# Shared expert over four PSUM banks each way, its down product three batches behind the gate

## The chip, the cores and the metric

The kernel runs on one NeuronCore of a Trainium2 chip. The core has five engines that matter here: TensorE (PE, matrix products, in the profile split into matmuls, PE, and weight loads, PEld), VectorE (DVE), ScalarE (ACT), GpSimd (POOL) and SyncE (SP, which only issues DMAs). Each engine works through its own list of instructions in order; semaphores order the engines against each other. PE writes its results to PSUM, eight banks of 512 fp32 numbers in each of 128 partitions; DVE and ACT read them from there. The metric is device microseconds from the start to the end of one execution.

## The reference

The input x has 32 batches of 128 tokens with 128 features. Four residual steps follow each other: a cross-attention with 16 heads of 8 features, a mixture of 8 experts (two per token), a cross-attention with 16 heads of 64 features, and a mixture of 16 experts (one per token) beside a shared expert that every token passes through. The change touches only the shared expert of the last step:

```python
logits = x @ w_router.T
_, top_idx = jax.lax.top_k(logits, 1)
...
expert_out = jnp.einsum('eth,ehf->etf', ...)        # the one expert that a token chose
shared = jax.nn.silu(x @ w_gate.T) * (x @ w_up.T) @ w_down.T
out = shared + expert_out.sum(axis=0)
```

Here x is the normalised input of the step, w_gate and w_up have 256 rows, and w_down turns 256 features back into 128.

## The kernel before

The program is written out by hand: every engine has one list, and the order in a list is the order of the calls in the source. P is 128, NB is 32 (the batches), LAST is 31. The stages follow each other: the first attention (to about 200 us in the trace), its experts (to 340), the second attention (to 745), the shared expert together with the routing of the second mixture (to 811), and the expert tiles (to the end).

**The shared expert, one batch b.** PE runs shared_gate(b) (line 1450): four fp32 matmuls of 128x128 into one PSUM bank, s_bank[b % 2]; the trace shows them as eight records, because an fp32 matmul is two instructions. The first two matmuls are the gate, the other two the upward product. ACT runs its own shared_gate(b) (line 1885): silu of the first half of the bank into sg[b % 2]. DVE runs product(b) (line 2443): sg times the second half of the bank into hT[b % 2]. PE runs shared_down(b) (line 1462): two matmuls (four records) from hT into the bank st_bank[1 - b % 2]. DVE runs add_shared(b) (line 2451): it adds that bank to x[:, b, :]. GpSimd then scatters the 128 rows of the batch with one indirect DMA (line 965) to buf1 in HBM, each row to the slot of its expert.

**The semaphores between them** are counters: g_full (gate done), sg_done (silu), sh_done (product), sy_full (down product), sy_done (sum). need(engine, semaphore, value) waits only for a positive value. Since there are two banks, gate b waits until the product of b-2 has read its bank, and down product b waits for the sum of b-2.

**The order of PE.** drain() (line 1485) ends the second attention and places the first gates and down products between the last transposes and logits. last_ranks() counts tokens per expert into the banks of and jf. Then a loop runs shared_gate(b) and shared_down(b - 2) for b from 4 to 33. Behind it PE runs warm(SCATTER_WARM), 20 matmuls whose result nobody reads, waits until all 32 scatters have landed (scattered), and runs warm(LOAD_WARM), eight more. Both write to the bank of.

**The order of DVE.** In drain() (line 2486) stand product(0) to product(2) among the norms and the choice of experts, then expert_slots() (line 2533) with product(3), add_shared(1), add_shared(2) and the arithmetic that gives each token its slot, then the loop product(b), add_shared(b - 1) for b from 4, and for b = 16 to 20 one step of tile_experts (line 2551) ahead of the product. expert_slots reads the banks of and jf.

**Behind the stage.** SP loads a quarter of the down weights of the experts, over the normalised rows xnFT, after each eight gates (line 729), and loads the first expert tiles from buf1 once all scatters have landed (line 731). DVE scales a tile by its score, PE transposes it, and the expert tiles begin: 47 of them, each with the same 8 and 4 matmul records as a batch here and one transpose, and one indirect DMA of GpSimd that stores it.

**Banks.** bank[0] to bank[3] are the four banks of sf, bank[4] and bank[5] the two of mf, and of and jf are a bank each. s_bank is bank 0 and 1, st_bank is bank 2 and 3, pj_bank is bank 4 and 5. The second bank of mf holds transposes and logits up to DVE's choose_last, which stands before product(2).

Of the kernel before, what the change touches and what calls it, by code (L numbers as in the profile page):

```python
# [9 lines left out]
ALU = mybir.AluOpType  # L10
ACT = mybir.ActivationFunctionType
AX = mybir.AxisListType

NB = 32
# [259 lines left out]
XRING, YRING, XSEMS = 20, 8, 6  # L274
DEEP = 4
XPARTS = 4
XB = NB // XPARTS
# [4 lines left out]
LAG0 = X0 + 4  # L282
DRAIN0 = 4


# [4 lines left out]
def build(nc, a, out):  # L290
    ctx = ExitStack()
    with ctx:
# [128 lines left out]
        xsT1 = [xsT[r // 2][:, r % 2, :] for r in range(DEEP)]  # L421
        hT1 = [hT[r // 2][:, :, (r % 2) * P:(r % 2 + 1) * P] for r in range(DEEP)]
        ysb1 = [rows[:, XRING + r, 0:DM] for r in range(YRING)]
        W0 = F0 + 2
# [28 lines left out]
        o_bank = [of[:, 0:QH * (D1 + 1)], mf[:, 0, 0:QH * (D1 + 1)]]  # L453
        g_bank, y_bank = bank[0:4], (of[:, 0:DM], jf[:, 0:DM])


# [85 lines left out]
        with nc.Block(no_gpsimd_drain=True) as block:  # L542
# [437 lines left out]
            def _(pe):  # L980
# [469 lines left out]
                def shared_gate(b):  # L1450

                    if b == 0:
                        pe.wait_ge(M1.w_in, 32)
                        pe.wait_ge(L1.exp_done, 2 * NB)
                    pe.wait_ge(L1.moved_done, MOVED1[b + 2] + 1)
                    need(pe, M1.sh_done, b - 1)
                    for c in range(4):
                        last = nc.tensor.matmul(s_bank[b % 2][:, c * P:(c + 1) * P], wgu[:, c * P:(c + 1) * P], xnFT[:, b, :],  # L1458
                                                start=True, stop=True)
                    last.then_inc(M1.g_full, 1)  # L1460

                def shared_down(b):
# [3 lines left out]
                    pe.wait_ge(M1.sh_done, b + 1)  # L1466
                    need(pe, M1.sy_done, b - 1)
                    for c in range(2):
                        last = nc.tensor.matmul(st_bank[1 - b % 2][:, 0:DM], hT[b % 2][:, c, 0:P], wdn[:, c, :], start=(c == 0),
                                                stop=(c == 1))  # L1470
# [14 lines left out]
                def drain():  # L1485
# [26 lines left out]
                    last_ranks()  # L1512
                    for b in range(4, NB + 2):
                        if inside(b):
                            shared_gate(b)
                        shared_down(b - 2)

# [86 lines left out]
                pe.wait_ge(slots_ready, NROUNDS + 3)  # L1604
                warm(SCATTER_WARM)
                pe.wait_ge(M1.scattered, 16 * NB)
                warm(LOAD_WARM)

# [36 lines left out]
            def _(act):  # L1645
# [239 lines left out]
                def shared_gate(b):  # L1885

                    act.wait_ge(M1.g_full, b + 1)
                    need(act, M1.sh_done, b - 1)
                    nc.scalar.activation(sg[b % 2][:, :, :], s_bank[b % 2][:, 0:2 * P], ACT.Silu).then_inc(M1.sg_done, 1)

# [88 lines left out]
            def _(dve):  # L1979
# [463 lines left out]
                def product(b):  # L2443

                    dve.wait_ge(M1.sg_done, b + 1)
                    need(dve, M1.sy_full, b - 1)
                    nc.vector.tensor_tensor(hT[b % 2][:, :, 0:P], sg[b % 2][:, :, :],
                                            s_bank[b % 2][:, 2 * P:4 * P].rearrange("p (c n) -> p c n", c=2),
                                            ALU.mult).then_inc(M1.sh_done, 1)

                def add_shared(b):

                    dve.wait_ge(M1.sy_full, b + 1)
                    nc.vector.tensor_tensor(x[:, b, :], x[:, b, :], st_bank[1 - b % 2][:, 0:DM], ALU.add).then_inc(M1.sy_done, 1)

# [30 lines left out]
                def drain():  # L2486
# [31 lines left out]
                    for b in range(4, NB):  # L2518
                        if NB // 2 <= b <= NB // 2 + 4:
                            tile_experts(b - NB // 2)  # L2520
                        product(b)
                        add_shared(b - 1)
                    add_shared(LAST)

# [220 lines left out]
```

## Time and profile before

| | us |
|---|---|
| median of three timed runs | 844.25 |
| lowest and highest | 844.01, 845.23 |
| span of the profiled execution | 913.6 |
| PE busy in it | 839.1 |
| DVE busy | 600.8 |
| ACT busy | 553.3 |
| POOL busy | 474.1 |

For the profiled execution only the span is known, from its first to its last instruction; it is longer than the timed runs. Each row of the trace has a start, a duration, the engine, the line of the source, the operation with output and inputs, and in brackets how long the engine had been idle before it and who released it. Starts on PE are recorded, the ends of matmuls are modelled. A row with x8 is eight instructions in a row, one overlapping the next. Indirect DMAs appear on POOL as the time that GpSimd needs to issue them; their landing is later.

### The profile page before, as it was taken

Reading aid. Unit: us, or ns where it says so; the run is one execution under the profiler, and the core shown is the slowest. Engines: PE = TensorE matmul, PEld = TensorE weight load, DVE = VectorE, ACT = ScalarE, POOL = GpSimd, SP = SyncE. Lnnn points to the kernel's source line nnn. Section 1 sums busy time; section 2 is a strip of 40 time slices with the busy share of each in tenths; the row PEclk is TensorE's granted clock in tenths of the full one; section 3 lists DMA queues with packets and bytes.
Section 4 is the critical chain, followed back from the end, with each engine's and each line's share of the span. In section 5 each row is a group of like instructions: output and inputs, shape, how many; then the busy total and the mean of one; then the engine's idle time right before and its main releaser. Section 6 shows DMA issues by size and latency. Waiting matters only on the chain.

```text
span 913.6 us, 31471 instructions
## 1 busy us (share of the span) xinstructions
PE 839.1 (92%) x11905; PEld 715.4 (78%) x11905; DVE 600.8 (66%) x1729; ACT 553.3 (61%) x1221; POOL 474.1 (52%) x575
## 2 busy tenths in 40 slices
PE   8998888878899998999999999999999998888786
PEld 3666555546589987998998998998999998867686
DVE  8886677734565647887777777677777676424343
ACT  4886676535387775776665666666666652225463
POOL 6333323463614436786656656655654444544455
PEclk9998999978799998999999999999999999999999
DMA  5455553513534432333553001001000002343330
GB/s 155 137 160 155 157 158 120 154 39 137 195 100 131 129 99 88 107 116 79 175 200 141 24 24 31 24 26 31 23 25 20 12 2 65 115 154 96 92 104 25
DMA packets 84148, 87.37 MB, mean 96 GB/s; under 512 B 15057, under 2 KB 70552, under 8 KB 83234
## 3 DMA queue, kind: packets, MB, share of 16 engines
q1 hardware_dynamic: 74946, 68.11, 24.7%
q0 software_dynamic: 8256, 17.01, 6.0%
q8 instruction: 99, 1.62, 0.7%
q14 instruction: 47, 0.39, 0.1%
q10 hardware_dynamic: 800, 0.24, 0.1%
HBM read 43.13 MB, written 40.44 MB: 91 GB/s over the span
## 4 chain that ended last, share of the span: by engine, by line
PE 81%; DVE 9%; issue 4%; ACT 2%; another core or an unknown queue 1%; DMA 1%; POOL 1%; SPq 0%; ACTq 0%; DVEq 0%; POOLq 0%
PE of L1367 8%; PE sf L1321 7%; PE jf L1242 6%; PE sf L1630 5%; PE sf L1283 4%; PE sf L1559 4%; PE mf L1269 4%; DVE cmx L2004 4%; PE jf L1251 3%; PE sf L1547 3%; PE sf L1458 3%; PE sf L1251 3%; PE of L1080 3%; PE sf L1033 2%; PE mf L1348 2%
## 5 line engine op out<-in xcount | busy, mean ns | idle before, releaser
L882 POOL TENSOR_TENSOR pl<-pT,ph 128x512 bf16<-128x512 f32 x128 | 146.1, 1165 | 105.1 <-DVE ph L2272 101.2
L806 POOL DMA_INDIRECT buf<-gu,slots x64 | 63.8, 996 | 88.9 <-PE of L1169 38.4
L2278 DVE TENSOR_REDUCE cmxb<-mf 128x8 bf16<-128x1024 f32 x64 | 78.2, 1222 | 43.6 <-PE mf L1348 39.2
L1700 ACT ACTIVATE pTf<-sf 128x1024 f32<-128x1024 f32 x64 | 62.6, 1022 | 36.6 <-PE sf L1040 18.0
L2004 DVE TENSOR_REDUCE cmx<-mf 128x8 bf16<-128x1024 f32 x64 | 78.1, 1220 | 10.0 <-PE mf L1061 6.8
L1818 ACT ACTIVATE pT<-sf 128x1024 f32<-128x1024 f32 x64 | 66.6, 1041 | 25.1 <-PE sf L1331 25.1
L1321 PE MATMUL sf<-qTs,kTs 64*128 64x128 f32 x1024 | 75.0, 286 | 1.6 <-ACT pT L1818 1.6
L871 POOL DMA_INDIRECT gb<-eo,slots x64 | 64.9, 1014 | 19.0 <-issue 18.9
L971 POOL DMA_INDIRECT out<-rows x47 | 46.3, 984 | 50.7 <-DVE rows L2677 39.7
L1321 PEld LDWEIGHTS sf<-qTs,kTs 64*128 64x128 f32 x1024 | 62.6, 188 | 7.1 <-issue 2.1
L1242 PE MATMUL jf<-wo,oT 128*128 128x128 f32 x496 | 62.9, 280 | 0.0
L1242 PEld LDWEIGHTS jf<-wo,oT 128*128 128x128 f32 x496 | 57.8, 192 | 0.0
L2263 DVE TENSOR_TENSOR o1s<-of,rden 128x256 f32<-128x256 f32 x125 | 53.1, 425 | 4.3
L1080 PE MATMUL of<-pTf,vq 128*32 128x128 f32 x1024 | 41.4, 290 | 12.6 <-issue 7.5
L1923 ACT ACTIVATE hT<-sf,qTs 128x128 f32<-128x128 f32 x142 | 44.6, 367 | 13.0 <-PE sf L1547 10.6
L2669 DVE TENSOR_TENSOR hT<-kTs,sf 128x256 f32<-128x256 f32 x47 | 19.8, 421 | 47.4 <-ACT kTs L1973 40.7
L1630 PE MATMUL sf<-xsT,qTs 128*128 128x128 f32 x376 | 49.7, 275 | 0.0
L861 POOL DMA_DIRECT2D eo<-rows x35 | 19.6, 561 | 52.2 <-DVE rows L2605 52.2
L1782 ACT CAST kTb<-mf 128x512 bf16<-128x512 f32 x24 | 14.1, 586 | 53.9 <-PE sf L1269 53.9
L1559 PE MATMUL sf<-dn,hT 128*128 x284 | 44.4, 279 | 1.9 <-DVE rows L2605 1.4
L1630 PEld LDWEIGHTS sf<-xsT,qTs 128*128 128x128 f32 x376 | 45.6, 191 | 0.0
L1547 PE MATMUL sf<-qTs 128*128 128x128 f32 x284 | 44.4, 279 | 0.1
(353 smaller groups left out, 2725.4 us busy)
## 6 DMA issues: line engine op xcount, KB each, us to landing
buf<-zero SPq DMA_DIRECT2D x12, 516.0 KB, 7.1
rows<-buf SPq DMA_DIRECT2D x47, 129.0 KB
buf<-zero SPq DMA_DIRECT2D x22, 256.0 KB, 3.8
eo<-zero SPq DMA_DIRECT2D x22, 256.0 KB
ctxT<-in_ctxP SPq DMA_DIRECT2D x24, 192.0 KB, 2.4
rows<-buf SPq DMA_DIRECT2D x71, 64.0 KB
gu<-in_gu SPq DMA_DIRECT2D x4, 1024.0 KB
kept<-kTs SPq DMA_DIRECT2D x6, 512.0 KB
```

The source lines that it names most:

```text
L871: nc.gpsimd.indirect_dma_start(out=gb[t % 4 * 2 + k][:, :], out_offset=None, in_=eo0[0:ZROW + P, :], in_offset=bass.IndirectOffsetOnAxis(a ...
L882: nc.gpsimd.tensor_tensor(pl[h][:, :, c, :], pT[h][:, :, c, :], ph[h][:, :, c, :], ALU.subtract)\
L1080: last = nc.tensor.matmul(of[32 * c:32 * c + 32, j * P:(j + 1) * P], vq[q % 2][:, u, h, :], pTf[p][:, h, :], start=True, stop=True)
L1242: last = nc.tensor.matmul(ps[:, 0:DM], oT[:, c, :], wo1[:, c, :], start=(c == 0), stop=(c == NCH - 1))
L1321: nc.tensor.matmul(S1[:, r, n * P:(n + 1) * P], kT[p][rr, 4 * h + n, :], qT[p][rr, 4 * h + n, :], start=(n == 0), stop=False)
L1367: last = nc.tensor.matmul(ps[:, j * (D1 + 1):(j + 1) * (D1 + 1)], pp[h][:, r, n, :], va1[p][part][:, QH * g + j, :], start=(m == 0), stop= ...
L1547: last = nc.tensor.matmul(s_bank[n % 2][:, f * P:(f + 1) * P], stage0[n % DEEP][:, f * P:(f + 1) * P], xsT0[n % DEEP], start=True, stop=True)
L1559: last = nc.tensor.matmul(st_bank[n % 2][:, 0:DM], hT1[n % DEEP][:, f, :], w2r[:, bass.ds(e, 1), f, :].squeeze(1), start=(f == 0), stop=(f ...
L1630: last = nc.tensor.matmul(g_bank[n % DEEP][:, c * P:(c + 1) * P], stage[n % DEEP][:, c * P:(c + 1) * P], xsT1[n % DEEP], start=True, stop= ...
L1818: nc.scalar.activation(pT[h][:, :, :, :].rearrange("p r c n -> p r (c n)"), S1, ACT.Exp, scale=D1 ** -0.5)\
L2004: nc.vector.reduce_max(to, mf[:, :, :].rearrange("p c (j k) -> p c j k", j=QH), AX.X)\
L2278: nc.vector.reduce_max(cmx1[b % 2][:, :].rearrange("p (r k) -> p r k", r=2)[:, :, 4 * h:4 * h + 4], M1p[:, :, :].rearrange("p r (c k) -> p ...
```

## The change

The gates get four PSUM banks and the down products four others, with slots that follow the batch number modulo four from batch 4 on and modulo two before. Products and silus get four buffers each: hT1, which the expert tiles use too, and sgs, the two old sg and two parts of pT[1]. The waits are counted accordingly: gate b waits for product b-4, from batch 8 on (6 and 7 wait for product 2). In PE's loop the down product stands three batches behind the gate. DVE adds batch b-3 behind product b, and the last three at the end; for b = 4 and 5 it adds nothing. The warm-up matmuls go to bank 0, since of is now a bank of the down products.

```diff
+BEHIND = 3
+def shared_slot(b):
+    return b % 4 if b >= 4 else b % 2
+def shared_before(b):
+    return b - 4 if b >= 8 else 2 if b >= 6 else b - 2
...
+        sgs = [t[:, :, :] for t in sg] + [pT[1][:, r, 0:2, :] for r in range(2)]
+        gs_bank = s_bank + pj_bank
+        sy_bank = [t[:, 0:DM] for t in (st_bank[1], st_bank[0], of, jf)]
...
-                    need(pe, M1.sh_done, b - 1)
+                    need(pe, M1.sh_done, shared_before(b) + 1)
                     for c in range(4):
-                        last = nc.tensor.matmul(s_bank[b % 2][:, c * P:(c + 1) * P], wgu[:, c * P:(c + 1) * P], xnFT[:, b, :],
+                        last = nc.tensor.matmul(gs_bank[shared_slot(b)][:, c * P:(c + 1) * P], wgu[:, c * P:(c + 1) * P], xnFT[:, b, :],
...
-                    need(pe, M1.sy_done, b - 1)
+                    need(pe, M1.sy_done, shared_before(b) + 1)
                     for c in range(2):
-                        last = nc.tensor.matmul(st_bank[1 - b % 2][:, 0:DM], hT[b % 2][:, c, 0:P], wdn[:, c, :], start=(c == 0),
+                        last = nc.tensor.matmul(sy_bank[shared_slot(b)], hT1[b % DEEP][:, c, :], wdn[:, c, :], start=(c == 0),
...
-                    for b in range(4, NB + 2):
+                    shared_gate(4)
+                    shared_down(2)
+                    shared_gate(5)
+                    for b in range(6, NB + BEHIND):
                         if inside(b):
                             shared_gate(b)
-                        shared_down(b - 2)
+                        shared_down(b - BEHIND)
...
-                warm(SCATTER_WARM)
+                warm(SCATTER_WARM, bank[0])
                 pe.wait_ge(M1.scattered, 16 * NB)
-                warm(LOAD_WARM)
+                warm(LOAD_WARM, bank[0])
...
-                    need(act, M1.sh_done, b - 1)
-                    nc.scalar.activation(sg[b % 2][:, :, :], s_bank[b % 2][:, 0:2 * P], ACT.Silu).then_inc(M1.sg_done, 1)
+                    need(act, M1.sh_done, b - DEEP + 1)
+                    nc.scalar.activation(sgs[b % DEEP], gs_bank[shared_slot(b)][:, 0:2 * P].rearrange("p (c n) -> p c n", c=2),
+                                         ACT.Silu).then_inc(M1.sg_done, 1)
...
-                    need(dve, M1.sy_full, b - 1)
-                    nc.vector.tensor_tensor(hT[b % 2][:, :, 0:P], sg[b % 2][:, :, :],
-                                            s_bank[b % 2][:, 2 * P:4 * P].rearrange("p (c n) -> p c n", c=2),
+                    need(dve, M1.sy_full, b - DEEP + 1)
+                    nc.vector.tensor_tensor(hT1[b % DEEP], sgs[b % DEEP],
+                                            gs_bank[shared_slot(b)][:, 2 * P:4 * P].rearrange("p (c n) -> p c n", c=2),
...
-                    nc.vector.tensor_tensor(x[:, b, :], x[:, b, :], st_bank[1 - b % 2][:, 0:DM], ALU.add).then_inc(M1.sy_done, 1)
+                    nc.vector.tensor_tensor(x[:, b, :], x[:, b, :], sy_bank[shared_slot(b)], ALU.add).then_inc(M1.sy_done, 1)
...
                         product(b)
-                        add_shared(b - 1)
-                    add_shared(LAST)
+                        if b >= 2 * BEHIND:
+                            add_shared(b - BEHIND)
+                    for b in range(NB - BEHIND, NB):
+                        add_shared(b)
```

## Rows read from the trace of the kernel before

**Rows 1.** The first line of the page: the span of the profiled execution.

```profile
span 913.6 us, 31471 instructions
```

**Rows 2.** Busy us by stretch: PE, PEld, DVE, ACT, POOL (instructions), PE clock, DMA share, GB/s.

```profile
400.00:744.00 344.00, 342.85 (x6154) 313.08 (x6147) 253.05 (x674) 222.24 (x458) 202.31 (x223) 1.00 0.20 60
763.00:811.00 48.00, 41.34 (x353) 39.53 (x351) 23.14 (x78) 10.94 (x29) 28.90 (x30) 1.00 0.34 113
820.00:911.00 91.00, 71.99 (x610) 68.48 (x608) 38.71 (x138) 48.06 (x137) 45.47 (x47) 1.00 0.31 86
```

**Rows 3.** In order of time, 773 to 780: PE, then ACT, DVE and POOL.

```profile
773.47 1.13 PE L1458 MATMUL sf<-dn,wgu 128*128 128x128 f32 x8 [1.01 <-DVE hT L2447]
774.43 0.61 PE L1469 MATMUL sf<-wdn,hT 128*128 128x128 f32 x4
...
776.22 1.06 PE L1458 MATMUL sf<-dn,wgu 128*128 128x128 f32 x8
777.11 0.61 PE L1469 MATMUL sf<-wdn,hT 128*128 128x128 f32 x4
...
774.63 0.38 ACT L1889 ACTIVATE sg<-sf 128x256 f32<-128x256 f32 x1 [1.46 <-PE sf L1458]
...
778.33 0.38 ACT L1889 ACTIVATE sg<-sf 128x256 f32<-128x256 f32 x1 [1.87 <-issue]
...
775.08 0.29 DVE L2454 TENSOR_TENSOR rows<-rows,sf 128x128 f32<-128x128 f32 x1 [1.23 <-issue]
775.28 0.41 DVE L2447 TENSOR_TENSOR hT<-sg,sf 128x256 f32<-128x256 f32 x1
...
779.06 0.29 DVE L2454 TENSOR_TENSOR rows<-rows,sf 128x128 f32<-128x128 f32 x1 [1.61 <-PE sf L1469]
...
775.79 0.96 POOL L965 DMA_INDIRECT buf<-rows,slot  x1 [0.30 <-issue]
...
779.63 0.96 POOL L965 DMA_INDIRECT buf<-rows,slot  x1 [1.27 <-DVE rows L2454]
```

**Rows 4.** First layer: stretches with the exponentials of L1700 alone, then its scatters.

```profile
30.00:75.00 45.00, 19.24 (x20) 1.00 0.53 154
...
89.00:190.80 101.80, 31.43 (x32) 0.92 0.47 141
...
L806 POOL DMA_INDIRECT buf<-gu,slots x16: 967/974/1210, 77.2 to 116.7; - x16
```

**Rows 5.** In order of time, the expert stage: two gates of PE in a row.

```profile
897.66 1.06 PE L1630 MATMUL sf<-xsT,qTs 128*128 128x128 f32 x8
...
899.11 1.06 PE L1630 MATMUL sf<-xsT,qTs 128*128 128x128 f32 x8
```

**Rows 6.** In order of time, PE in the shared stage: gates alone.

```profile
765.13 1.13 PE L1458 MATMUL sf<-dn,wgu 128*128 128x128 f32 x8
...
768.20 1.13 PE L1458 MATMUL sf<-dn,wgu 128*128 128x128 f32 x8 [1.50 <-issue]
...
769.61 1.06 PE L1458 MATMUL sf<-dn,wgu 128*128 128x128 f32 x8
...
770.95 1.06 PE L1458 MATMUL sf<-dn,wgu 128*128 128x128 f32 x8
...
787.64 1.06 PE L1458 MATMUL sf<-dn,wgu 128*128 128x128 f32 x8
...
789.19 1.13 PE L1458 MATMUL sf<-dn,wgu 128*128 128x128 f32 x8
```

**Rows 7.** In order of time, DVE: slot arithmetic, product 4, a tile-table step, a product.

```profile
766.88 0.62 DVE L2530 TENSOR_REDUCE v<-wk 128x28 f32<-128x448 f32 x1
...
767.64 0.41 DVE L2447 TENSOR_TENSOR hT<-sg,sf 128x256 f32<-128x256 f32 x1
...
788.05 0.54 DVE L2555 TENSOR_TENSOR pT<-rowno,upto 1x384 f32<-1x384 f32 x1
788.62 0.42 DVE L2447 TENSOR_TENSOR hT<-sg,sf 128x256 f32<-128x256 f32 x1
```

**Rows 8.** In order of time: POOL at scatters 4 and 31, PE's warm-ups, the first tile loads.

```profile
770.86 0.96 POOL L965 DMA_INDIRECT buf<-rows,slot  x1 [0.53 <-issue]
...
813.83 0.96 POOL L965 DMA_INDIRECT buf<-rows,slot  x1 [0.30 <-issue]
...
811.21 4.48 PE L986 MATMUL of<-ones 128*128 128x512 bf16 x20
...
816.36 2.70 SPq L736 DMA_DIRECT2D rows<-buf  x6
...
816.38 1.90 PE L986 MATMUL of<-ones 128*128 128x512 bf16 x8 [0.69 <-DMA buf<-rows,slot]
```

## The prediction

> **What bounds the kernel now.** I read the first line of the page, then the busy time by stretch, then the instructions in order of time of each engine in the stretch that the change touches. The profiled execution spans 913.6 us [rows 1], yet the median of the timed runs is 844.25: the profiled one took 69.4 us more. All durations below are of the profiled execution, so the first question is which of its waits exist in a timed run at all.
>
> In attention PE is busy 342.85 of 344 us at full clock [rows 2]: nothing to lose there. In the shared-expert stretch, 763 to 811, it is busy 41.34 of 48, in the expert stage behind it 71.99 of 91 [rows 2]. The idle PE time there has a mark of its own. In an undisturbed batch the silu starts 1.16 us after its gate (773.47 to 774.63). The gate issued at 776.22 follows its predecessor without a pause, but its silu starts at 778.33, 2.11 us later, and the sum of the down product issued at 777.11 starts 1.95 us later (779.06) [rows 3]. PE had dispatched the work; what came late was its signal, to ACT and DVE alike. At that time GpSimd issues one scatter after another (775.79), and the next one, at 779.63, waits for the late sum [rows 3]. The same shows in the first layer: 20 exponentials (10 batches) in 45 us, 4.5 us a batch, before any scatter; the first scatter comes at 77.2; from 89.0 to 190.8 there are 32 exponentials, 6.36 us a batch [rows 4]. And the 47 expert tiles take 1.94 us each where two gates in a row stand 1.45 apart [rows 2, 5]. Against the undisturbed paces that is 101.8 - 16 x 4.5 = 29.8 us, 91 - 47 x 1.45 = 22.9 us, and, as worked out below, 7.0 us for the shared stage: 59.7 us, 86% of the 69.4 us that the profiled run took longer. I conclude that late signals beside indirect DMAs belong mostly to the profiled execution. What counts for the time is the schedule without them.
>
> The Trainium skill ("Perfetto Trace Analysis", Tensor Engine Instruction) says that a matmul's signal goes out only when PSUM has acknowledged its bytes, behind the window that the profiler draws; by that rule, the rows agree: starts are on time and signals are not. The skill ("NOTIFIC — the notification-queue block", 7.1) says the records' own pipeline can push back on an engine; no row here shows whether it did.
>
> **The schedule of before, without late signals.** PE per batch: 8 gate records and 4 down records; starts 1.34 us apart (769.61 to 770.95), 0.89 of it the gate, and 1.41 behind a wait (768.20 to 769.61) [rows 6]. A gate at T gives a silu at T + 1.16, a product that ends at about T + 2.2 (775.28 + 0.41, issued behind the sum) [rows 3]. Gate b+2 is due at T + 2.68 and needs that product: some 0.5 us to spare, so the loop runs at PE's pace except in two places. (1) Product 4 stands behind the slot arithmetic (one instruction of 0.62 among it), starts at 767.64, and PE waits 1.50 us until gate 6 at 768.20 [rows 6, 7]. (2) Each tile-table step puts 0.54 ahead of a product (788.05, product at 788.62), and gate 18 to 19's stretch shows 0.2 of idle: 787.64 + 1.34 = 788.98, issued 789.19 [rows 6, 7]; the stall itself makes room for the next step, so of four steps I count two, 0.4. Gate 31 is then at 769.61 + 24 x 1.34 + 0.4 = 802.17; down product 29 at 803.06; its sum starts 0.65 later (774.43 to 775.08) and lasts 0.29; GpSimd starts 0.28 behind a sum's end (779.35 to 779.63) [rows 3]: scatter 29 at 804.28. Scatters follow each other in 0.96 + 0.30 = 1.27 [rows 8]: scatter 31 at 806.8, where the profile has 813.83 [rows 8]. Difference 7.0, the figure used above. Everything behind hangs on the last scatter: it lands, the tile loads go out (816.36), the second warm-up starts (816.38) [rows 8].
>
> **The change, part by part.** Arithmetic, bytes and instructions stay; the last waits of the stage are re-aimed.
> - Four gate banks and four product buffers: gate 6 now needs product 2, not 4, and gate b needs b-4. The 1.50 goes: gate 5 at 765.13 [rows 6], gate 6 at 766.10, down 3, gate 7 at 767.44, gate 8 at 768.78 (before: 770.95). Down 4, at 768.33, needs product 4 (767.64 + 0.41 [rows 7]): just there. The 0.4 of the tile steps goes too, since slack grows from 0.5 to over 2.5 us. Gate 31 at 768.78 + 23 x 1.34 = 799.60, 2.57 earlier.
> - Down product three behind: three down products (29, 30, 31) now stand behind the last pair instead of two, 0.45 each, so the last sum ends only about 2.3 us earlier. More important is GpSimd: the sums of 28 to 31 arrive faster than it scatters. Down 28 at 800.49, its sum at 801.14, or behind product 31 at about 801.6, ends 801.9; scatter 28 at 802.15 and scatter 31 three periods later, 805.95 (805.7 if the sum goes first). The queue's own floor from scatter 4 (770.86 [rows 8]) is 770.86 + 27 x 1.27 = 805.1, so GpSimd takes back most of what PE gains.
> - DVE: for b = 4 and 5 there is no sum beside the product; sum 3 moves behind product 6, about 768.8, and scatter 3 is due at 769.36 (770.86 less 1.50): still in time. DVE is busy 23.14 of 48 [rows 2]; free.
> - ACT: the same silu into other buffers, 0.38 each [rows 3]; two of them lie in pT, unused here. I take 0. The nearest other ACT row shapes are alike, so -0.01 to +0.01 a batch, hidden.
> - Banks mf, of and jf: of and jf are first used by down 6 and 7, behind the reads of the ranks (sum 3's wait); mf by gates 6 and 7, behind product 2, which DVE issues after the last choice. No row shows a cost of another bank: 0, between -0.1 and +0.1 in all.
> - Warm-up into bank 0: same 20 and 8 matmuls, 4.48 us for the 20 [rows 8]. It starts 2.3 us earlier, the landing comes 0.9 earlier.
> - SP loads the down weights when gates 8, 16, 24 and 32 are done, at most 2.6 us earlier: nobody waits earlier.
>
> Sum: last scatter 806.8 to 805.85, -0.95 us, passed on to the end one to one: 844.25 - 0.95 = 843.3. With size errors (the tile steps 0 to 0.8, product 31 ahead or not, scatter pace) -0.3 to -2.0.
>
> **Rivals.**
> - Late signals exist in the timed runs too. Then before pays up to 7.0 more, and the changed loop, with 2.5 us and more of slack against lateness of 1.0 to 1.3 (2.11 - 1.16, 1.95 - 0.65), does not stall; it keeps about 1 us of lateness at scatter 28. Full size: 813.83 to about 806.9, 844.25 - 6.9 = 837.3. Half size: about 840.5. For: the marks are plain in the trace. Against: 86% of the missing time.
> - Slower: the clock. PE's last warm-up matmul ends at about 806.7, the landing is at 805.85 + 2.5 = 808.4: 1.7 us idle, where before had 0.69 [rows 8]. If the clock falls to 1.2 GHz there, the expert stage starts at half speed: 3 to 5 tiles of 1.45 us of PE work [rows 5] cost as much again, minus PE's idle share there, +2 to +4 against -0.95: 845.3 to 847.3. It decides from a loss over 1 us on. Against: the stage ran at clock 1.00 with a 1.50 idle in it [rows 2, 6]. The skill ("TensorE: Matmul & The Clock Gate", Efficiency of idle gaps under Part 1) warns of PE idle between bursts.
> - Scatter queue alone decides. If a timed scatter loop of before already ran at its floor, 805.1, since the first stall is shorter there, the extra queued scatter costs 0.6 to 0.9: 844.9 to 845.1.
> - It does not do what it says: nothing moves because GpSimd bounds the stage throughout; then 844.2, inside the main range.
>
> **How the numbers follow.** Small gain as worked out: 0.60. Late signals real at half size 0.18, at full size 0.10. Clock 0.06. Queue alone 0.06. Likeliest time 843.3, its own range 842.2 to 844.2. The range to hold 8 in 10 reaches to the half-size case and its lower side and over the queue case: 838.5 to 845.3. A measurement of this kernel can tell about 0.2%, 1.7 us, from no change. Faster by more: 0.28 + 0.07 of the small case = 0.35. Slower by more: 0.06 and some of the queue case = 0.08. Within: 0.57.
>
> **What would show it.** In the profile of the changed kernel: no wait before gate 6, gates 1.34 apart from gate 6 to 31 and none waiting for a product; silus still up to 1 us late, harmless; GpSimd nearly without a pause to the last scatter, four scatters back to back at the end; span 6 to 7 us shorter although the time is only 1 us shorter; clock 1.00 through the warm-ups. Wrong, if the time falls by as much as the span: then late signals are real. Wrong too, if PE still waits for products in the loop, or if the last scatter starts less than 0.3 us earlier against the gates' start than my schedule says.

## The result, and the profile after

The changed kernel takes 841.62 us (median of five executions, 840.31 to 842.72), the kernel before in the same comparison 844.25 (843.41 to 845.23). The ratio is 0.9968, with a 95% interval of 0.9956 to 0.9981: a gain of 2.6 us, between 1.6 and 3.7. The forecast was 843.3, a gain of 0.95. All medians here and below are of executions in the fast state of the chip; one execution of the kernel "three behind, two banks" fell in a slower state (890.01 us, mean granted clock 0.957) and is left out.

The profiled execution of before that stands ahead of the prediction was a disturbed one (span 913.6 [rows 1], its timed runs 844). The one of after was not, so the two stages can't be subtracted. The kernel before, run again without an edit, gives the fair partner; it is the first experiment below.

The first line of the page of after; its own time was 841.63:

```profile
span 839.9 us, 31468 instructions
```

Busy us by stretch of after, with the columns of [rows 2] (PE, PEld, DVE, ACT, POOL with instructions, clock, DMA share, GB/s):

```profile
400.00:700.00 300.00, 299.96 (x5447) 274.32 (x5443) 221.85 (x595) 193.84 (x398) 172.09 (x189) 1.00 0.17 51
716.50:757.00 40.50, 40.24 (x361) 39.30 (x357) 23.58 (x79) 10.88 (x29) 29.15 (x31) 1.00 0.43 137
766.00:838.00 72.00, 68.14 (x607) 67.57 (x606) 43.25 (x138) 48.87 (x136) 46.13 (x47) 0.99 0.39 108
```

In the shared stage PE is now busy 40.24 of 40.5 us, where [rows 2] had 41.34 of 48. The same stretch of the undisturbed kernel before:

```profile
716.50:757.00 40.50, 38.56 (x344) 37.69 (x342) 23.27 (x77) 10.76 (x28) 27.99 (x30) 1.00 0.40 128
```

Gates of PE in after, in order of time (compare [rows 6]):

```profile
719.52 1.06 PE L1472 MATMUL mf<-dn,wgu 128*128 128x128 f32 x8
720.41 0.61 PE L1483 MATMUL sf<-wdn,hT 128*128 128x128 f32 x4
720.86 1.06 PE L1472 MATMUL mf<-dn,wgu 128*128 128x128 f32 x8
721.75 0.61 PE L1483 MATMUL sf<-wdn,hT 128*128 128x128 f32 x4
722.20 1.06 PE L1472 MATMUL sf<-dn,wgu 128*128 128x128 f32 x8
...
753.02 1.06 PE L1472 MATMUL mf<-dn,wgu 128*128 128x128 f32 x8
```

Gates 6 to 8 (719.52, 720.86, 722.20) stand 1.34 apart without a bracket, and so do all up to gate 31 (753.02). The stall of 1.50 before gate 6 is gone.

The sum of batch 14 on DVE, then GpSimd in after, scatter 14 and scatters 27 to 31, and PE's two warm-ups behind the stage (compare [rows 8]):

```profile
736.16 0.28 DVE L2472 TENSOR_TENSOR rows<-rows,of 128x128 f32<-128x128 f32 x1
737.44 0.96 POOL L979 DMA_INDIRECT buf<-rows,slot  x1 [1.01 <-DVE rows L2472]
...
754.08 0.96 POOL L979 DMA_INDIRECT buf<-rows,slot  x1 [0.38 <-DVE rows L2472]
755.42 0.96 POOL L979 DMA_INDIRECT buf<-rows,slot  x1 [0.38 <-DVE rows L2472]
756.69 0.96 POOL L979 DMA_INDIRECT buf<-rows,slot  x1 [0.30 <-issue]
757.96 0.96 POOL L979 DMA_INDIRECT buf<-rows,slot  x1 [0.31 <-issue]
759.22 0.96 POOL L979 DMA_INDIRECT buf<-rows,slot  x1 [0.30 <-issue]
```

```profile
755.70 4.48 PE L1000 MATMUL sf<-ones 128*128 128x512 bf16 x20
762.13 1.90 PE L1000 MATMUL sf<-ones 128*128 128x512 bf16 x8 [1.95 <-DMA buf<-rows,slot]
```

The first scatter is at 718.89, so first to last takes 40.33 us. Most scatters follow each other at 1.27. Scatters 25 to 28 (up to 755.42) wait for their sums and come 1.34 apart, at PE's pace; 29 to 31 come 1.27 apart without a wait. Ahead of scatter 14 stands an odd gap of 1.97, caught up by scatter 25: its sum ends at 736.44 and it starts 1.00 later, at 737.44, where a scatter that waits only for its sum starts some 0.27 behind it. PE idles 1.95 before the second warm-up, and the clock stays at 1.00.

### The profile page after: what moved, and what is told of

The parts are those of the page before. It is cut to its first block, busy times and chain, and to the rows that moved or that the text cites. A ratio compares the mean times of both kernels' runs of the same rounds, so it can differ in the third digit from the quotient of the medians.

```text
span 839.9 us, 31468 instructions
## 1 busy us (share of the span) xinstructions
PE 806.0 (96%) x11905; PEld 701.2 (83%) x11905; DVE 608.6 (72%) x1729; ACT 555.6 (66%) x1221; POOL 475.4 (57%) x575
## 4 chain that ended last, share of the span: by engine, by line
PE 82%; DVE 9%; issue 4%; POOL 3%; DMA 1%; ACT 1%; SPq 1%; POOLq 0%; DVEq 0%
PE of L1381 8%; PE sf L1335 8%; PE jf L1256 7%; PE sf L1297 4%; PE mf L1283 4%; PE sf L1576 4%; PE sf L1564 4%; PE jf L1265 4%; DVE cmx L2022 4%; PE sf L1647 3%; PE sf L1265 3%; PE sf L1047 2%; PE of L1094 2%; PE mf L1362 2%; PE mf L1075 2%
## 5 line engine op out<-in xcount | busy, mean ns | idle before, releaser
L1047 PE MATMUL sf<-rows,kTq 32*128 32x512 f32 x256 | 41.1, 644 | 0.8 <-ACT cT L1759 0.4
L2614 DVE COPY qTs<-gu 128x258 f32 x71 | 21.3, 303 | 27.7 <-ACT hT L1941 26.8
```

## The experiments

The experiments ran in three groups of four, on three different chips of the same kind: "before again", "banks only", "three behind" and "product 4 first" on the first, "changed, again", "closer end" and the two half kernels on the second, those of the last part on the third. On which chip the first comparison ran (the row "changed kernel") is not on record. "Before beside it" is the kernel before, timed together with the kernel of the row. In the tables "stage" is first to last scatter, "gates" is gate 4 to gate 31, "behind" is last scatter to the end of the trace, all of one profiled execution.

| kernel | median us | before beside it | 95% interval of the ratio | stage | gates | behind |
|---|---|---|---|---|---|---|
| before again | 842.98 | 843.63 | 0.9980 to 1.0005 | 41.50 | 38.77 | 80.39 |
| changed kernel | 841.62 | 844.25 | 0.9956 to 0.9981 | 40.33 | 36.04 | 80.65 |
| changed, again | 841.77 | 844.09 | 0.9947 to 0.9984 | 40.32 | 36.04 | 80.30 |
| banks only | 841.63 | 843.63 | 0.9969 to 0.9998 | 39.98 | 37.26 | 80.39 |
| three behind, two banks | 867.02 | 843.63 | 1.0266 to 1.0328 | 65.36 | 60.9 | |
| product 4 first | 842.55 | 843.63 | 0.9978 to 1.0005 | 40.87 | 38.14 | |
| closer end | 842.94 | 844.09 | 0.9959 to 0.9996 | 40.13 | 36.49 | 80.63 |
| half gates | 841.03, one | | | 39.31 | | 81.84 |
| half scatters | 841.47, one | | | 39.34 | 36.04 | 81.35 |

### The kernel before again

No edit.

> The kernel before, unchanged, profiled once more. If late signals beside indirect DMAs belong to a disturbed profiled execution, its span is about 842.6 us (1.7 below its time, as for the changed kernel), every silu starts 1.16 us after its gate, and the only question left is how long the stage takes: from the first to the last scatter 41.3 us if my schedule was right (40.3 in the changed kernel, so 1.0 gained), 43 if the measured 2.6 us come from this stage. Rival: the signals are late in every execution of this order of work; then the span is near 913 again and the scatters take 48 us.

PE around gate 6, and the end of the stage in GpSimd's list:

```profile
719.99 0.61 PE L1469 MATMUL sf<-wdn,hT 128*128 128x128 f32 x4
722.09 1.13 PE L1458 MATMUL sf<-dn,wgu 128*128 128x128 f32 x8 [1.50 <-DVE hT L2447]
723.50 1.06 PE L1458 MATMUL sf<-dn,wgu 128*128 128x128 f32 x8
```

```profile
758.32 0.96 POOL L965 DMA_INDIRECT buf<-rows,slot  x1 [0.38 <-DVE rows L2454]
759.59 0.96 POOL L965 DMA_INDIRECT buf<-rows,slot  x1 [0.30 <-DVE rows L2454]
760.85 0.96 POOL L965 DMA_INDIRECT buf<-rows,slot  x1 [0.30 <-issue]
```

The span is 841.3. The same 1.50 stands before gate 6. Of the tile-table steps two cost 0.2 each (gaps of 1.55 and 1.54 before gates 18 and 20 instead of 1.34), and every other gate from 7 on comes 1.34 to 1.42 behind its predecessor. No silu comes late: from gate 4 on each starts 1.09 to 1.18 behind its gate, the larger values behind a gate that had waited. The stage takes 41.50 us where the prediction's schedule had 41.34, and where the disturbed execution had 48.37.

### Which half of the change brings it

Banks only: the down product two behind and the sum one behind, as before.

```diff
-                    shared_gate(4)
-                    shared_down(2)
-                    shared_gate(5)
-                    for b in range(6, NB + BEHIND):
+                    for b in range(4, NB + 2):
...
-                        shared_down(b - BEHIND)
+                        shared_down(b - 2)
...
-                        if b >= 2 * BEHIND:
-                            add_shared(b - BEHIND)
-                    for b in range(NB - BEHIND, NB):
-                        add_shared(b)
+                        add_shared(b - 1)
+                    add_shared(LAST)
```

> Changed kernel, but the down product stays two batches behind the gate and the sum one behind the product, as before; four banks and four buffers are kept. My theory: the banks carry the whole gain, PE has no wait from gate 6 on, and with one scatter less queued at the end it is 0.4 to 0.9 us faster than the changed kernel, about 841.0; from the first to the last scatter 39.5 to 39.9 us. Rival: the third batch of distance is what gives the slack; then this kernel is at 843 to 844.5 with waits for products in the loop.

```profile
720.08 1.06 PE L1472 MATMUL mf<-dn,wgu 128*128 128x128 f32 x8
721.64 0.71 PE L1483 MATMUL sf<-wdn,hT 128*128 128x128 f32 x4 [0.51 <-DVE hT L2462]
722.19 1.06 PE L1472 MATMUL mf<-dn,wgu 128*128 128x128 f32 x8
```

One stall is left, which the expectation did not have: down 4 waits for product 4, and gate 7 comes 2.11 behind gate 6. PE therefore reaches gate 31 about 1.2 us later than in the changed kernel (37.26 against 36.04), yet the last scatter is not later: 39.98 against 40.33, since here two scatters queue at the end and not three. The time, 841.63, is that of the changed kernel. So the banks alone bring a gain (between 0.2 and 2.6 us by the interval), and the third batch of distance adds none that can be measured; the two kernels were not timed beside each other here, only on the third chip, where neither gains.

Three behind with two banks: the converse.

```diff
-                    for b in range(4, NB + 2):
+                    shared_gate(4)
+                    shared_down(2)
+                    shared_gate(5)
+                    for b in range(6, NB + 3):
...
-                        shared_down(b - 2)
+                        shared_down(b - 3)
...
+                        if b >= 6:
+                            add_shared(b - 3)
                         product(b)
-                        add_shared(b - 1)
-                    add_shared(LAST)
+                    for b in range(NB - 3, NB):
+                        add_shared(b)
```

> Kernel before with two banks and two buffers each, but the down product three batches behind the gate. My theory: product b now waits until down product b-2 has read the buffer, which stands behind gate b+1; product b ends at T + 3.3 where gate b+2 is due at T + 2.68: 0.6 to 0.7 us of wait per batch, 15 to 20 us slower, about 861. Rival (distance alone helps): within 1 us of the kernel before or faster.

One round of the loop, all engines:

```profile
736.12 0.61 PE L1469 MATMUL sf<-wdn,hT 128*128 128x128 f32 x4
736.32 0.38 ACT L1892 ACTIVATE sg<-sf 128x256 f32<-128x256 f32 x1 [1.87 <-PE sf L1458]
736.84 0.42 DVE L2450 TENSOR_TENSOR hT<-sg,sf 128x256 f32<-128x256 f32 x1 [1.63 <-PE sf L1469]
737.17 0.28 DVE L2457 TENSOR_TENSOR rows<-rows,sf 128x128 f32<-128x128 f32 x1
737.40 1.13 PE L1458 MATMUL sf<-dn,wgu 128*128 128x128 f32 x8 [0.67 <-DVE hT L2450]
```

The product waits for the down product before it, since hT has only two buffers, and the next gate waits for that product: down product at 736.12, product 0.72 later, gate 0.56 behind that. Each round takes 2.25 us instead of 1.34. The three executions have a median of 867.02, 23.4 us above the kernel before; the expectation had 861, since it sized a round's wait at 0.6 to 0.7 where it is 0.91. In the traces the stage is 23.9 longer than in the kernel before: 22.1 of it between gates 6 and 31 (25 rounds of 2.25 against 34.13 us) and 1.7 behind gate 31. The distance needs the buffers; they don't need it.

### One stall alone

Product 4 stands ahead of the last slot arithmetic; all else as before.

```diff
                     add_shared(2)
+                    product(4)
                     dve.wait_ge(scored, NQD)
...
-                        product(b)
+                        if b > 4:
+                            product(b)
```

> Kernel before, product 4 moved ahead of the slot arithmetic of 28 batches on DVE. This takes the 1.5 us wait before gate 6 away, but product 5 stays behind the arithmetic and makes gate 7 wait about 0.5. My theory: 0.8 to 1.2 us less wait on PE, all of it passed on: 843.1 to 843.5. Rival: GpSimd's queue, not PE, decides when the last scatter goes; then within 0.3 us of the kernel before.

```profile
721.90 1.06 PE L1458 MATMUL sf<-dn,wgu 128*128 128x128 f32 x8
722.79 0.61 PE L1469 MATMUL sf<-wdn,hT 128*128 128x128 f32 x4
724.27 1.13 PE L1458 MATMUL sf<-dn,wgu 128*128 128x128 f32 x8 [0.87 <-DVE hT L2447]
```

The wait before gate 6 (721.90) is gone, and gate 7 (724.27) now waits 0.87 for product 5, where 0.5 was expected. In all PE waits 0.63 less than the 1.50 of before, and 0.63 is what the stage gets shorter (41.50 to 40.87). So a stall of PE at the start of the loop is passed on to the last scatter at full size when PE paces the loop. In the times, 842.55 to 843.63, its interval just includes no change.

### GpSimd's queue

Closer end: the changed kernel, from batch 22 on two behind again, so that fewer scatters queue at the end.

```diff
+CLOSER = 22
...
-                        shared_down(b - BEHIND)
+                        if b <= CLOSER:
+                            shared_down(b - BEHIND)
+                        if b >= CLOSER:
+                            shared_down(b - 2)
```

> Changed kernel with the distance of three only up to batch 22 and two from there on (two down products stand behind gate 22), so the start skips the wait for product 4 and the end queues one scatter less. My theory: from the first to the last scatter 39.8 to 40.0 us, 0.3 to 0.5 less than the changed kernel, and as much in the time. Rival: the queue at the end costs nothing because GpSimd is at its floor anyway; then 40.3 again.

The stage shortens by 0.20 (40.33 to 40.13), where 0.3 to 0.5 was expected; it now ends at GpSimd's own pace from the gap ahead of scatter 14 on, but for one gap of 1.40. The time, 842.94, is not lower than that of the changed kernel beside it, 841.77. Five of its twelve executions, and one of the changed kernel's, had a mean granted clock below 0.9895; what that does to a median stands in the part on the size of the whole, below. What there is to win at the end is too small to see.

Half gates: the changed kernel with only the gate half of the four gate matmuls; the upward product is left out, and the product uses the gate half twice.

```diff
-                    for c in range(4):
+                    for c in range(2):
...
-                                            gs_bank[shared_slot(b)][:, 2 * P:4 * P].rearrange("p (c n) -> p c n", c=2),
+                                            gs_bank[shared_slot(b)][:, 0:2 * P].rearrange("p (c n) -> p c n", c=2),
```

> Changed kernel with only the first two of the four gate matmuls of each batch; the product multiplies the silu by the same half of the bank, so the shared expert's upward product is left out. PE needs 0.89 us a batch instead of 1.34. My theory: GpSimd's queue bounds the changed stage; from the first to the last scatter 39.3 to 40.0 us, against 40.33 with all gates. Rival: PE bounds it; then about 12 us less until the last scatter.

Busy us by stretch, and PE's two warm-ups:

```profile
744.00:762.00 18.00, 6.65 (x28) 2.72 (x27) 0.46 (x2) 1.14 (x2) 11.06 (x12) 0.69 0.39 136
762.00:775.00 13.00, 12.88 (x97) 11.13 (x96) 6.48 (x21) 8.83 (x25) 3.22 (x4) 0.90 0.51 141
```

```profile
744.13 4.48 PE L1000 MATMUL sf<-ones 128*128 128x512 bf16 x20
759.96 3.59 PE L1000 MATMUL sf<-ones 128*128 128x512 bf16 x8 [11.35 <-DMA buf<-rows,slot]
```

PE is done 11.6 us earlier (744.13 against 755.70), and first to last scatter still takes 39.31 us: that is GpSimd's own pace, 31 periods of 1.27. The changed kernel's 40.33 lies 1.0 above it, and that is the most that can still come from PE, DVE and ACT in this stage.

Half scatters: the changed kernel without the scatters of the odd batches (their rows are left out of buf1).

```diff
+                    if b % 2:
+                        continue
...
-                pe.wait_ge(M1.scattered, 16 * NB)
+                pe.wait_ge(M1.scattered, 16 * NB // 2)
```

> Changed kernel without the scatters of the odd batches (left out; their rows stay empty). PE, ACT and DVE do all their work. My theory: GpSimd's queue is what the end waits for; with 16 scatters it is empty when the last sum is there, scatter 30 starts 0.3 behind its sum, 37.0 to 37.3 us after the first scatter, and the expert stage starts 3 us earlier. Rival: PE's last down product sets the end, and only the 0.4 us between the sums of 30 and 31 are gained.

```profile
753.41 0.96 POOL L981 DMA_INDIRECT buf<-rows,slot  x1 [1.72 <-DVE rows L2474]
757.15 0.96 POOL L981 DMA_INDIRECT buf<-rows,slot  x1 [2.79 <-DVE rows L2474]
758.42 0.96 POOL L981 DMA_INDIRECT buf<-rows,slot  x1 [0.30 <-issue]
```

```profile
752.37 0.28 DVE L2474 TENSOR_TENSOR rows<-rows,of 128x128 f32<-128x128 f32 x1
755.05 0.48 DVE L2474 TENSOR_TENSOR rows<-rows,sf 128x128 f32<-128x128 f32 x2
```

With no queue the scatters follow the sums, 2.68 apart, up to the 14th, which starts 0.76 behind the end of its sum (752.65 to 753.41), as those before it do. The 15th, of batch 28, has its sum at about 755.34 (the first of the two instructions at 755.05) and starts 1.8 us later, at 757.15. I did not expect that; the last section comes back to it. Because of it this run can't say what the last scatter would be without a queue: it came 39.34 us behind the first, where 37.0 to 37.3 was expected.

### Everything once more, on a third chip

The last four ran together. Each fully timed one was executed twelve times, the kernel before 29 times.

| kernel | median us (lowest, highest) | 95% interval of the ratio | stage | gates |
|---|---|---|---|---|
| kernel before | 904.05 (898.66, 910.44) | | | |
| changed | 904.92 (900.56, 910.74) | 0.9985 to 1.0039 | 47.11 | 39.38 |
| banks only | 903.61 (895.94, 906.65) | 0.9965 to 1.0014 | 46.31 | 42.77 |
| banks and product 4 first | 904.29 (901.91, 906.37) | 0.9972 to 1.0019 | 46.86 | 42.12 |
| changed, 16 more instructions on GpSimd | 901.3, one | | 46.40 | 38.68 |

On this chip every execution of every kernel took some 60 us more (895.94 at the least), and the change gains nothing: between 1.4 us faster and 3.5 us slower. "Banks only" and "changed" are the kernels from above word for word. "Banks and product 4 first" joins two edits already shown. The fourth puts 16 small memsets ahead of GpSimd's first scatter:

```diff
                 attention()
+                for r in range(16):
+                    nc.gpsimd.memset(xrn[0][:, 2 * r:2 * r + 2], 0.0)
                 pool.wait_ge(zeroed[1], 16 * NZERO[1])
```

> The changed kernel, word for word, so that it stands in the same call as e9_banks_product4 and e10_banks_again. Expected 841.7, ratio 0.997 to the kernel before; first to last scatter 40.3 us.

> The kernel of e2_banks_only once more, word for word, beside the changed kernel in the same call. If being three behind is worth nothing, the time stands within 0.6 us of the changed kernel and at 0.997 of the kernel before; if it is what brings the gain, the time lies 1 us or more above the changed kernel. In the trace: first to last scatter 40.0 us again, one gap of 2.1 us between gates 6 and 7.

> The four banks with the down product two batches behind (as in e2_banks_only), and product 4 moved in the list of DVE ahead of the last slot arithmetic (as in e4_product4_first). In e2_banks_only the loop had one stall left, 0.77 us before gate 7, since down product 4 waited for product 4. Theory that waits for products are all that PE loses: that stall goes, all gates from 6 on stand 1.34 apart, gate 4 to gate 31 takes 36.2 us, but the slots of the last batches come about 0.4 later. The queue of GpSimd then decides: first to last scatter 39.5 to 40.2 us, time within 0.8 us of the changed kernel. Rival (the lateness of the slots costs more than the stall did): a gap of 1.7 us or more at scatter 2 to 4 and a last scatter no earlier than in e2_banks_only, 40.0 to 40.9 us, and time as in e4_product4_first, 842.5.

> The changed kernel, with 16 memsets of two columns more in the list of GpSimd ahead of the first scatter (output unchanged). In the traces so far the gap ahead of the 15th scatter is 0.2 to 1.4 us longer than its sum explains, also where only every second batch is scattered. Theory A (the position in the list of instructions decides): the gap moves to an earlier scatter, some 5 to 12 scatters earlier, and the 15th stands at 1.27. Theory B (the number of scatters before it decides, as where a ring of descriptors comes round): the gap stays ahead of the 15th, 1.5 to 2.1 us. Theory C (the time since the stage began decides): it stays at about 737 us. The time: within 0.5 us of the changed kernel in all three.

The expectations had counted on the times and stages of the first two chips, and for these they can't be tested here. The one stall can: in "banks only" gate 7 again comes 2.11 behind gate 6 (755.35 to 757.46), and with product 4 first as well it comes 1.34 behind (761.68 to 763.02), as expected.

The marks that the prediction read from the disturbed execution are here in their full size. PE, ACT and GpSimd of the changed kernel on the third chip:

```profile
span 902.7 us, 31468 instructions
```

```profile
772.24 1.06 PE L1472 MATMUL mf<-dn,wgu 128*128 128x128 f32 x8
...
776.47 0.27 PE L1472 MATMUL sf<-dn,wgu 128*128 128x128 f32 x1 [0.61 <-issue]
...
777.90 0.27 PE L1483 MATMUL of<-wdn,hT 128*128 128x128 f32 x1 [0.81 <-issue]
778.01 1.05 PE L1472 MATMUL mf<-dn,wgu 128*128 128x128 f32 x8
```

```profile
773.67 0.39 ACT L1906 ACTIVATE pT<-mf 128x256 f32<-128x256 f32 x1 [2.52 <-PE mf L1472]
777.95 0.38 ACT L1906 ACTIVATE pT<-mf 128x256 f32<-128x256 f32 x1 [3.89 <-PE sf L1472]
```

```profile
775.67 0.96 POOL L979 DMA_INDIRECT buf<-rows,slot  x1 [0.39 <-DVE rows L2472]
779.26 1.02 POOL L979 DMA_INDIRECT buf<-rows,slot  x1 [2.63 <-DVE rows L2472]
```

PE starts gate 15 at 772.24, and its silu runs at 777.95, 5.71 us later; undisturbed it is 1.09. Between the silus at 773.67 and 777.95 lie 4.28 us without one. There are four such stops in this stage, of 3.6 to 4.3 us, ending some 10 us apart; the lags behind them reach 3.81, 5.71, 4.71 and 4.47 (gates 8, 15, 23 and 29), and then shrink by about a microsecond a batch. In the disturbed trace of the kernel before, the largest lag was 2.32. That its two banks kept the lag small, by stopping PE soon, is an argument and not shown: no trace of the kernel before on the third chip exists. With four banks PE runs ahead, and its gates take 39.38 us instead of 44.43. But each sum behind a stop is late all the same, GpSimd has nothing to scatter in that time (2.63 idle before 779.26), and its own period of 1.27 is too close to PE's 1.34 to catch up. Five microseconds won on PE become 1.3 at the last scatter (48.37 to 47.11, one execution each), and 0 in the time.

For the order of the four kernels nothing can be read from this chip: their intervals overlap. The run with 16 more instructions on GpSimd has its long gaps where they are without the memsets (ahead of scatters 5, 11 and 12, 19 and 25), so the stops don't go by the position in GpSimd's list. Nor does the hitch at scatter 14. Scatter 13, the sum of batch 14 and scatter 14 with the memsets:

```profile
778.38 0.96 POOL L981 DMA_INDIRECT buf<-rows,slot  x1 [0.30 <-issue]
778.72 0.28 DVE L2474 TENSOR_TENSOR rows<-rows,of 128x128 f32<-128x128 f32 x1
780.00 0.96 POOL L981 DMA_INDIRECT buf<-rows,slot  x1 [0.66 <-issue]
```

The sum ends at 779.00, scatter 13 leaves GpSimd free at 779.34, and scatter 14 starts at 780.00: 0.36 later than the usual 0.30 behind its predecessor, and again 1.00 behind its sum. Without the memsets it is 782.20 behind a sum that ends at 781.20, 1.00 too. That fits theory B (the gap stays at the 15th scatter), and neither A (it moves to an earlier one) nor C (it stays at about 737 us).

## Why the prediction was right, and where it was not

**The reading of a disturbed profile held for these timed runs, not in general.** The prediction took late signals out of the schedule because the profiled run was 69.4 us longer than the timed ones. In the trace of after and in those of the first two chips there are none; of the 72.3 us between the two spans of before (913.6 and 841.3), 46.1 lie ahead of the stage's first scatter, 6.9 in the stage and 19.4 behind it. The stage's 7.0 was right, the 22.9 for what is behind it 3.5 too high, and the 29.8 covered only a part of what is ahead. What was too narrow is the sentence that late signals belong mostly to the profiled execution. On the third chip all executions have the long span, and each of the four traces from it shows them; the profile ahead of the prediction may well come from such a chip, and its timed runs from another, which the numbers at hand then could not tell.

**The schedule of before** had 41.34 us from first to last scatter, measured 41.50; of after 40.39 (40.49 with product 31 ahead of the sum), measured 40.33. The predicted 0.95 became 1.17. (The prediction's other value, 805.7 with the sum first, should be 805.5 by its own terms, and its half-size case 840.8, not 840.5; neither decides anything.) Gate 31 of after was due 34.14 behind the first scatter and came at 34.13; from scatter 28 to 31 it was 3.80 in both. The stall of 1.50 and the tile steps of twice 0.2 were as worked out, and all are gone. PE gains 2.73 (38.77 to 36.04, predicted 2.57), and 1.56 of it is lost again up to the last scatter: 1.27 since one scatter more stands in GpSimd's queue behind the last sum it had to wait for, 0.3 since sum 28 stands behind product 31 on DVE. "Banks only" shows the queue too: with PE 1.2 us slower the last scatter is no later.

**The size of the whole** was too small: 0.95 against 2.6, with 1.6 as the least that the interval allows. The measured 841.62 lies outside the range that the prediction gave its own case (842.2 to 844.2) and nearer to the half-size case of its rival (840.5) than to 843.3. It lies inside 838.5 to 845.3 because two rivals had stretched that range, which is luck; what speaks for the small case and against the rival is the traces, not the time. The changed kernel once more, beside 23 executions of before, was 2.3 us lower (1.4 to 4.5 by the interval). I had expected 0.8 to 1.4 of that run from the traces, and 2.2 to 3.0 from its rival, that something outside the stage pays the rest.

In the two undisturbed traces the spans differ by 1.4: 0.5 ahead of the first scatter, which the change doesn't touch, 1.17 in the stage, -0.3 behind it. The second trace of after has the stage at 40.32 again. Over all executions on undisturbed chips the medians are 843.81 (67) and 841.66 (17), 2.2 apart. A part of the rest goes with the clock: the mean granted clock varies from execution to execution between 0.984 and 0.996. In the traces of the complete kernels on these chips the difference is the length of the pieces at 0.50 in the first layer, 6.8 us in the changed kernel's (mean 0.994) and 17.1 us in all in that of "product 4 first" (mean 0.988). Of executions with a mean clock of at least 0.9925 the medians are 843.27 (29) and 841.63 (13), 1.6 apart. Below 0.9895 lay 18 of the 62 of before whose clock is known, at a median of 845.3, and one of after's 17. That this is the draw and not the change is likely, since "banks only" and "closer end", with the same four banks, have 4 and 5 such executions of 12. So 1.2 us are shown in the stage; where the other 0.4 of the 1.6 come from no trace shows.

**Its signs.** No wait before gate 6, gates 1.34 apart, scatters 28 to 31 back to back and the clock at 1.00 through the warm-ups came as announced; silus up to 1 us late did not. The span fell by 73.7 us and not by 6 to 7, since the profile of after was not disturbed; so the sign that was to tell real late signals from others, span against time, could not be read from this pair.

**The rivals.** Late signals real: they are, on the third chip, and the price was wrong. The step that failed is that the changed loop, "with 2.5 us and more of slack against lateness of 1.0 to 1.3 (2.11 - 1.16, 1.95 - 0.65), does not stall" and keeps "about 1 us of lateness at scatter 28". The 1.0 to 1.3 had been measured on the loop of before; in the changed one on the third chip lateness reached 4.6 (5.71 less 1.09), its gates took 3.3 us longer than undisturbed (39.38 against 36.04), and its stage 6.8 (47.11 against 40.33). And the sum was made for PE alone, though the last scatter needs every sum. Forecast 6.9 us, measured none: between 1.4 faster and 3.5 slower. The clock: PE idles 1.95 before the second warm-up (1.7 was expected; 1.56 in the second trace of after), and the clock stays at 1.00. With half gates it idles 11.35, and the granted clock is 0.50 from 754 to 764 (0.69 over the row from 744 to 762), which is 1.2 GHz, and 1.00 again from 766 on. The eight warm-up matmuls take 3.59 instead of 1.90, and from the last scatter to the end it takes 81.84 us instead of 80.3 to 80.65: 1.2 to 1.5 more, where the rival had 2 to 4. The half-speed piece fell mostly on the warm-up matmuls, so 3 to 5 slow tiles were too many. The scatter queue alone, and nothing moves: the loop of before did not run at GpSimd's floor, since its scatters 19 to 29 stand 1.34 apart, so the first falls, and the interval of the ratio excludes the second.

The Trainium skill ("TensorE: Matmul & The Clock Gate", HAM oscillation — how this bites in real kernels; the prediction gave another name for the section) says that waits between bursts of matmuls put TensorE back to its low clock. The traces agree for the wait of 11.35 us and show none of it for the one of 1.95.

## What to carry to other kernels

Four banks are worth having where one instruction out of line stops a loop of two, and they need no greater distance in the order; distance without buffers costs the whole latency in each round (0.91 of 1.34 here). Before adding slack to an engine, look at the queue behind it: with GpSimd's period at 1.27 and PE's at 1.34, no more than 1 us of the changed stage is left to win, and 1.56 of the 2.73 that PE gained did not reach the last scatter. Lateness measured on a loop that stalls need not hold for one that stalls less (1.0 to 1.3 there, up to 4.6 here); and a profile of a disturbed execution can be read for its schedule, but whether the disturbance is the execution's or the chip's, only another chip tells.

## What the runs showed of the hardware

Three chips of one kind ran the same program at 844, 844 and 904 us. The 60 us do not lie in one place. In the shared stage PE's signals stop for 3.6 to 4.3 us about every 10 us, beside GpSimd's indirect DMAs; attention, where PE is busy 342.85 of 344 us [rows 2] and 342.90 on the third chip, loses nothing. In the stop shown above PE itself pauses twice (0.61 and 0.81 us ahead of 776.47 and 777.90), waiting for nothing that the profile shows. What stops the signals is open.

Scatter 14, the 15th indirect DMA of the stage, starts 0.99 to 1.01 us behind the end of its sum in eleven of the fourteen traces, where a scatter that waits only for its sum starts 0.26 to 0.28 behind it. (In the disturbed trace of before, one of the eleven, the queue alone would give the same.) What shows as its gap depends on how long the queue would have held it anyway: 0.7 us more than usual in before and after, 0.2 to 0.3 in "product 4 first" and "banks only", none in "half gates", where its sum had been ready for 4.44 us, nor in "banks only" on the third chip (1.15). In "half scatters", where the 15th is batch 28, it starts 1.8 behind its sum and the others 0.76. So it goes by the number of scatters: not by the batch, not by the time (735.95 to 787.29 us in the other thirteen traces), and, as far as 16 more instructions can tell, not by the place in GpSimd's list. What it is that takes 0.7 us more at the 15th is open.
